# Recurrent layer, 2 slices of 1024 tokens on each of 8 cores: one half's norm beside the other half's products, two sums written out for quadrant 12, s and x fetched in fours, and TensorE on zeros at the start

## The reference

```python
x = L0_attn_x
xn = _layernorm(x, axis=-1)
s = _L0_attn_ref(xn, L0_attn_input_weights, L0_attn_xis, L0_attn_proj_matrix)
g = _silu(_L0_ffn_ref(xn, ...))
x = x + s * g

def _L0_attn_ref(x, input_weights, xis, proj_matrix):
    def _rfs(xw, ab, AB, gs):
        dot_products = jnp.einsum('...d,rd->...r', xw, ab[:, None] * gs)
        correction = (0.5 * jnp.sum(xw * xw, axis=-1))[..., None] * (ab * ab)
        return 1.0 / math.sqrt(NUM_RFS) * AB * jnp.exp(dot_products - correction)
    ab = xis
    AB = jnp.exp(xis)
    weights = _rfs(input_weights, ab, AB, proj_matrix)
    feats = _rfs(x, ab, AB, proj_matrix)
    return jnp.einsum('bsr,or->bso', feats, weights)

def _L0_ffn_ref(x, w1_w, w1_s, w2_w, w2_s, h1_w, h1_s, h2_w, h2_s, w3_w, w3_s):
    h = jax.nn.silu(_tlin(x, w1_w, w1_s)) * _tlin(x, w2_w, w2_s)
    h = jax.nn.gelu(_tlin(h, h1_w, h1_s), approximate=False)
    h = jax.nn.gelu(_tlin(h, h2_w, h2_s), approximate=False)
    return _tlin(h, w3_w, w3_s)
```

## Time and profile before

| | |
|---|---|
| median of 3 runs | 2441.12 us (2439.59 to 2442.6) |
| the profiled execution | 2439.11 us |
| its span on the slowest core, core 4 | 2438.0 us |
| spans of the eight cores | 2417.9 to 2438.0 us |
| busy: PE, DVE, ACT, POOL | 2358.3, 1118.9, 416.8, 220.8 us |

### The profile page before, as it was taken

The page is one execution under the profiler, slowest core; times in us unless marked ns, Lnnn a source line. Parts: engine busy times, 40 slices in busy tenths (PEclk is TensorE's granted clock), DMA queues, the critical chain, the costliest instruction groups (busy, mean ns, idle before and its releaser), DMA issues.

```text
span 2438.0 us, 29505 instructions; the slowest of 8 cores (2417.9 to 2438.0 us)
## 1 busy us (share of the span) xinstructions
PE 2358.3 (97%) x10832; PEld 1062.0 (44%) x10832; DVE 1118.9 (46%) x1269; ACT 416.8 (17%) x589; POOL 220.8 (9%) x390
## 2 busy tenths in 40 slices
PE   6999999999999999999799999999999999999968
PEld 2444444444444444444344444444444444444423
DVE  4433443444744444563640433444443744343556
ACT  2212111111111111112422222111111111111111
POOL 1000000000000001011030000000000000000000
PEclk8999999999999999999999999999999999999989
DMA  7543455555655555678411643465656564656675
GB/s 139 95 79 69 72 92 92 93 91 95 119 86 99 95 90 99 128 136 125 109 70 70 104 75 65 74 103 82 106 81 105 105 107 81 106 82 103 124 172 121
DMA packets 78717, 240.01 MB, mean 98 GB/s; under 512 B 8304, under 2 KB 20208, under 8 KB 77552
## 3 DMA queue, kind: packets, MB, share of 16 engines
q0 software_dynamic: 57120, 192.96, 49.4%
q1 hardware_dynamic: 21456, 45.17, 5.8%
HBM read 408.49 MB, written 22.54 MB: 177 GB/s over the span
## 4 chain that ended last, share of the span: by engine, by line
PE 89%; DVE 6%; DMA 3%; ACT 1%; issue 1%; SPq 0%; DVEq 0%; ACTq 0%; POOLq 0%
PE pb L157 86%; PE pb L316 2%; DMA blk<-s_hbm 2%; DVE tmp L605 1%; DMA wring<-w3p 1%; ACT blk L609 1%; DVE blk L259 1%; DVE blk L253 1%; DVE wring L352 1%; SPq L742 0%; DVE blk L481 0%; DVE blk L501 0%; DVE blk L475 0%; DMA blk<-xT 0%; DVE blk L628 0%
## 5 line engine op out<-in xcount | busy, mean ns | idle before, releaser
L157 PE MATMUL pb<-blk,wring 128*128 128x512 bf16 x9856 | 2133.3, 379 | 29.8 <-DVE wring L352 18.8
L157 PEld LDWEIGHTS pb<-blk,wring 128*128 128x128 bf16 x9856 | 964.4, 98 | 1198.4 <-issue 40.6
L352 DVE TENSOR_TENSOR wring<-wring 128x2048 bf16<-128x2048 bf16 x216 | 264.7, 1226 | 50.6 <-DVE tmp L411 16.5
L297 DVE SCALAR_TENSOR_TENSOR blk<-pb,cols,stg 128x512 bf16<-128x512 f32 x128 | 96.0, 750 | 291.7 <-PE pb L157 208.5
L359 DVE TENSOR_TENSOR wring<-wring 128x2048 bf16<-128x2048 bf16 x144 | 176.4, 1225 | 15.4 <-DVE blk L501 0.5
L452 ACT ACTIVATE blk<-pb,cols 128x512 bf16<-128x512 f32 x64 | 44.0, 687 | 680.2 <-DVE tmp L404 680.2
L157 PE MATMUL pb<-blk 128*128 128x512 bf16 x640 | 140.9, 383 | 17.1 <-ACT blk L609 17.1
L452 ACT ACTIVATE blk<-tmp,cols 128x512 bf16<-128x512 f32 x128 | 92.4, 722 | 350.1 <-DVE tmp L411 175.9
L292 ACT ACTIVATE stg<-pb,cols 128x512 bf16<-128x512 f32 x128 | 88.0, 688 | 337.2 <-PE pb L157 298.7
L183 POOL DMA_DIRECT2D wring<-h1p x128 | 67.9, 531 | 740.2 <-PE pb L157 740.2
L183 POOL DMA_DIRECT2D wring<-h2p x128 | 67.9, 531 | 710.2 <-PE pb L157 688.2
(11 more groups left out here) (67 smaller groups left out, 512.1 us busy)
## 6 DMA issues: line engine op xcount, KB each, us to landing
wring<-h1p POOLq DMA_DIRECT2D x128, 512.0 KB, 5.8
wring<-h2p POOLq DMA_DIRECT2D x128, 512.0 KB, 6.0
wring<-w12p POOLq DMA_DIRECT2D x64, 512.0 KB, 5.7
wring<-w3p POOLq DMA_DIRECT2D x32, 512.0 KB, 9.3
blk<-xT SPq DMA_DIRECT2D x32, 256.0 KB, 6.1
y<-blk SPq DMA_DIRECT2D x32, 256.0 KB, 2.5
blk<-xT POOLq DMA_DIRECT2D x16, 256.0 KB, 17.8
s_hbm<-blk SPq DMA_DIRECT2D x16, 256.0 KB, 2.1
```

The source lines that it names most:

```text
L157: ii = t.matmul(p[bk], lhs, rhs, start=(not onto and i == 0), stop=(i == n - 1), skip_group_check=onto)
L297: a = V(lambda: v.scalar_tensor_tensor(kt(h[q], row), p[b2], w2s_c[:, oc:oc + 1], stg[:, ts_, :], op0=ALU.mult, op1=ALU.mult), m2, a)
L352: tok = V(lambda: v.tensor_add(wring[:, so, :], wring[:, slots[ka][0], :], wring[:, slots[kb][0], :]), *toks, slots[ka][1], slots[kb][1])
```

## The change

- *Norm at the start.* The three steps of `ln_scale` become `ln_mean`, `ln_var` and `ln_rstd`, and squares and statistics are called pair by pair. A new function `head0`, given to `w12_stage` for the first slice, interleaves the norm of half 1 with the first products of half 0: three chunks in four passes, each on the two tiles of xn that are there, then chunks 3 to 6 of half 0, then chunks 0 to 6 of half 1. The second slice has no special pass: all chunks go one by one.
- *PE on zeros.* `eb` is set to 0, and 24 matmuls on it run before x has landed.
- *Norm between the slices.* Half 0's center and divide stand beside the 128 products for the input weights, one operation for every two of them; half 1's statistics follow those products, and its center and divide stand beside the y products, one for each tile. The center writes to `stg`. s of the second slice is made half by half.
- *Quadrant 12.* A tile in `stg` is combined on the spot with quadrants 22 and 11 into its tiles of M3 and M6 (`sums_out`), and both go to HBM; the last two row groups write them straight to their blocks (`sums_here`). In the last row group two DMAs of 14 tiles each bring M6 (after the first unit) and M3 (after the second) back.
- *s5* is formed after quadrant 22 of a row group, not before.
- *End.* x and s come in groups of four tiles each, in the order of use; tile 14 is finished at once.

```diff
-        def ln_scale(th, f0, f1, f2):
+        def ln_mean(th, f0, f1, f2):
 
             bm, bv = ln[th, "banks"]
-            a = S(lambda: sc.activation(f1, p[bm], AF.Square), ln[th, "q"])
-            c = V(lambda: v.tensor_sub(f1, p[bv], f1), a)
+            ln[th, "f"] = (f0, f1, f2)
+            a = V(lambda: v.tensor_copy(f0, p[bm]), ln[th, "q"])
+            free_bank(bm, a)
+            ln[th, "m2"] = S(lambda: sc.activation(f1, f0, AF.Square), a)
...
+            def head_chunks(n, jj, banks_):
+
+                need(t, ln[0, "xn", jj])
...
+                for i in range(n):
+                    need(t, slots[key(i)][1])
...
+            first = head(chunk, head_chunks, gate) if head else 0
+            for i in range(first):
+                ch = chunk(i, 1)
+                gate(*ch)
+                give_slot(key(i), ch[5])
...
@@ row_group
             free_bank(ba, emit("12", r, p[ba], v2))
-            if nxt:
-                weight_sums(*nxt, "s5")
...
             t_free[2 * par] = emit("22", r, ta, a)
             if nxt:
+                weight_sums(*nxt, "s5")
                 weight_sums(*nxt, "s1")
@@ hidden_stage
+            def sums_out(r):
+
+                i = 2 * (r % 2)
+                a = V(lambda: v.tensor_sub(stg[:, i + 1, :], stg[:, i, :], kt(o22, r)),
+                      o_tok["12", r], o_tok["22", r], now(d_stg[i + 1]))
+                need(sy, a)
+                d_stg[i + 1].inc(sy.dma_start(spill[s_, nm, "M3"][:, r, :], stg[:, i + 1, :]), 16)
+                a = V(lambda: v.tensor_add(stg[:, i, :], stg[:, i, :], kt(o11, r)), o_tok["11", r])
+                need(sy, a)
+                d_stg[i].inc(sy.dma_start(spill[s_, nm, "M6"][:, r, :], stg[:, i, :]), 16)
...
-            def sum_m3():
-                V(lambda: v.tensor_sub(most(nb["M3"]), most(nb["M6"]), most(o22)),
-                  end["u1"], end["r12"])
...
+            def fetch(op, m):
+                need(sy, m, *[now(d) for d in d_stg])
+                reload_tok[op] = d_rel[op].inc(sy.dma_start(blk[:, nb[op], 0:14 * N], spill[s_, nm, op]), 16)
@@ the start
+        for _ in range(24):
+            t.matmul(p[7], ones_d, eb[:, 0, :], start=True, stop=True)
...
+        def head0(chunk, head_chunks, gate):
+
+            bk = []
+            head_chunks(3, 0, bk)
+            ln_stats(1, b_x, b_q, 3)
+            head_chunks(3, 1, bk)
+            ln_mean(1, *lnf[3:6])
+            ln_center(0, b_x, ft[0], 2)
+            ln_divide(0, b_xn, ft[0], 2)
+            ln_var(1)
+            ln_rstd(1)
+            head_chunks(3, 2, bk)
...
+            ch = head_chunks(3, 3, bk)
...
+            for jj in range(3):
+                c = chunk(3 + jj, 0)
+                if jj < 2:
+                    ln_center(1, b_x, ft[1], 2 + jj)
+                ln_divide(1, b_xn, ft[1], 1 + jj)
+                gate(*c)
+            gate(*chunk(6, 0))
@@ beside the input weights' products
-                    ln_center(rc // 4, b_x, ftl, rc % 4)
-                    ln_divide(rc // 4, b_xn1, ftl, rc % 4)
+                    if rc % 2 == 0:
+                        ln_center(0, b_x, ftl, rc // 2)
+                    else:
+                        ln_divide(0, b_xn1, ftl, rc // 2)
@@ the end
-                for n_ in range(8):
-                    x_load(n_, end["u4"])
-                need(sy, end["u5"], end["u6"], now(d_s))
-                sr = [d_sr[i].inc(sy.dma_start(f32b(b), s_hbm[:, 8 * i:8 * i + 8, :]), 16)
-                      for i, b in enumerate((fr1, fr2))]
+                def load(n0, x_after, s_after):
+
+                    need(sy, *x_after)
+                    for n_ in range(n0, n0 + 4):
+                        rows, cs, oc, th = where(*order[n_])
+                        d_xf[n_ % 8].inc(sy.dma_start(xf[:, n_ % 8, :], xT[rows, cs]), 16)
+                    need(sy, *s_after)
+                    for n_ in range(n0, n0 + 4):
+                        rows, cs, oc, th = where(*order[n_])
+                        in_tok[n_] = d_xf[n_ % 8].inc(
+                            sy.dma_start(sv[n_], s_hbm[:, 2 * oc + th, :]), 16)
+
+                in_tok = {}
+                load(0, [end["u4"]], [end["u5"], now(d_s)])
```

More of the change, by code:

```diff
@@ L111, in build_nc @@
         d_s = Ctr(nc, stack, "d_s")
-        d_sr = [Ctr(nc, stack, f"d_sr{i}") for i in range(2)]
         waited = {}
@@ L219, in ln_squares @@
             cs = slice(th * N, (th + 1) * N)
-            for jj in range(4):
-                js = slice(2 * jj, 2 * jj + 2)
-                ln[th, "sq", jj] = S(lambda: sc.activation(xq[:, js, cs], xb[:, js, cs], AF.Square),
-                                     ln[th, "x", jj], *toks)
-        def ln_stats(th, b, bq):
-            xb, xq = wide(b), wide(bq)
-            cs = slice(th * N, (th + 1) * N)
-            need(t, ones_tok)
-            bm, bv = take_bank(), take_bank()
-            for j in range(8):
-                need(t, ln[th, "sq", j // 2])
+            if jj == 0:
+                need(t, ones_tok)
+                ln[th, "banks"] = (take_bank(), take_bank())
@@ L337, in w12_stage @@
+            first = head(chunk, head_chunks, gate) if head else 0
[3 more added lines that the diff above has]
+                give_slot(key(i), ch[5])
+                if i % 2 == 1:
+                    sums(i // 2)
+            for i in range(first, 32):
+                for th in range(2):
+                    ch = chunk(i, th)
+                    gate(*ch)
+                give_slot(key(i), ch[5])
                 if i % 2 == 1:
@@ L485, in edge_last @@
                 if u == 0:
-                    need(sy, m, *[now(d) for d in d_stg])
-                    end["r12"] = d_rel.inc(sy.dma_start(most(nb["M6"]), spill[s_, nm][:, 0:15, :]), 16)
+                    fetch("M6", m)
+                elif u == 1:
+                    fetch("M3", m)
                 elif u == 2:
@@ L647, in build_nc @@
                     x_load(n_, s_, f_last)
-                ln_stats(0, b_x, b_q)
-                ln_stats(1, b_x, b_q)
+                for jj in range(4):
+                    ln_stats(0, b_x, b_q, jj)
                 need(t, iw_sq)
```

297 lines of the change are left out of this document (168 added, 129 removed).

## The result

The changed kernel takes **2403.35 us**, the median of four executions (2401.37, 2401.82, 2404.88 and one of 2688.45), and in the same session the kernel before takes 2441.86 (2439.59 to 2445.34). The ratio is **0.9838, 95% interval 0.9819 to 0.9858**: 1.6% faster. The range of 2379 to 2407 holds it; the forecast was 2392.5.

What follows compares the result with a forecast made beforehand. TensorE bounds the kernel: busy 97%, 2336.5 us of matmuls as floor, 101.5 us of waits or slow clock. Gains 8.3 + 23.7 + 0 + 15.4 + 1.2 = 48.6 gave 2390.5 profiled, 2392.5 median, range 2379 to 2407.

Steps and rivals of the forecast that it cites:

- head: Start of the first slice: half 0's products begin with its first norm tile; gain 8.3 us, bounds 5 to 12.
- middle: Between the two token slices: half the centers and divides move beside the y products; gain 23.7 us, 0.5 left.
- last stage: Second slice's w3: the wait for s goes, 7.4 us left of 22.8; gain 15.4 us, bounds 5 and 22.8.
- rival 2: Changes of stage: second reload is dear, fourth weight 8 us or more late; 2407 us in all, chance 0.17.
- a break above 8 us at a change of stage: Sign in the profile after that would make the sum wrong: PE breaks above 8 us where one stage follows another.
- h1 to h2: Change of stage, both slices: 2 us lost to the fourth weight where 1.7 and 2.0 were; net 0, twice.
- h2 to w3: Change of stage: first slice net 0, PE stopped 4.88 before; second slice 4.0 us idle plus 2.4 slow restart.
- tail: After the last products: two of four DVE steps of 0.7 to 0.9 us go; gain 1.2 us.
- Changes of stage: Four places: two block sums go, a second reload delays the fourth weight 4 to 5 us; gain 0.
- Rival 1: Changes of stage and last stage: the second reload costs nothing; 2380 us in all, chance 0.13.
- The rule against the row: Skill's two-port DVE rule, set aside: it would blame block sums for late fourth weights and make the second reload free.
- Rivals 3 and 4: 3: middle stays shut, 2410 us, chance 0.08; 4: chip withholds 2.4 GHz, slower than before, 2463 at 0.97, chance 0.03.

Runs made afterwards that it cites:

- the deferral: Changed kernel with xn's block and projT fetched after the third unit of w3's second row group, not at the end of h2; 2393.09 us.
- the spread kernel: Changed kernel with M3's reload after the fifth unit, xn and projT fetched in w3's second row group, s5 before quadrant 22 in the last stage alone; 2385.06 us.

## Why the prediction was right, and which terms were off

The sign and the range held, and the gains came where the prediction put them, in the head, the middle and the last stage; the sum was 11.3 us too fast (2401.8 against 2390.5). The range holds the result because it was drawn to take in rival 2. Of the signs named ahead, one of those against the sum came: a break above 8 us at a change of stage (9.56). By its own terms, on core 5 of after:

| term | left or gained by the prediction | in the trace | too fast by |
|---|---|---|---|
| head | gain 8.3 | 5.1 | 3.2 |
| middle | gain 23.7 | 24.2 | -0.5 |
| h1 to h2, first slice | 2 left | 2.74 + 1.9 slow | 2.7 |
| h1 to h2, second slice | 2 left | 0 | -2.0 |
| h2 to w3, first slice | 4.9 + 2.6 left | 9.56 + 2.9 slow | 5.0 |
| h2 to w3, second slice | 4.0 + 2.4 left | 6.33 + 2.9 slow | 2.8 |
| row groups of w3 | 1 left | 0.69 + 0.79 + 0.69 | 1.2 |
| tail | gain 1.2 | 0.5 | 0.7 |

That makes 13.1 for the 11.3; the 1.8 over is not accounted for, and the rows of before are core 4's, those of after core 5's. "Slow" is what a run of matmuls behind a stop takes over 0.2157 each: 94 in 22.14 (20.3 due), 121 in 28.95 (26.1), 112 in 27.04 (24.2).

**Changes of stage: the step that failed.** The prediction took 4 to 5 us for the second reload, "as part of the traffic is through by then", and nothing in the first slice's change to w3. The price is 6.5 us on the slowest cores (24.7 against 18.2) and 5.0 to 8.1 by the medians at the four changes. The second slice agrees: issued at 2272.48, landed at 2294.05, 21.6 us, where before the same weight took 15.3. For what the prediction said was through by then the trace has no sign: the DMA share is 1.02 in the window from 1015 to 1047, with 253 GB/s. 1.66 MB more in 6.5 us are 3.9 us for each MB.

The sum had priced the reload, which moves bf16 as it is, like weights, whose MB it counted in f32. The page of after has the two apart (queue, packets, MB as they land, share of 16 engines' span); POOL's casting transfers are q0, SP's are q1:

```profile
q0 software_dynamic: 57120, 192.96, 47.7%
q1 hardware_dynamic: 31536, 58.81, 7.5%
```

That is 5.9 us of all 16 engines for each MB that lands by q0 and 3.1 by q1 (2400.8 x 0.477 / 192.96 and x 0.075 / 58.81). An estimate from it is 1.66 x 3.1 = 5.1 us, the low end of what was measured. The prediction's 3.2 us for an MB is near the 3.1 only because a weight's MB of f32 lands as half an MB.

And xn's and projT's places were taken as given, while the deferral shows that their 4 MB make 7.5 of the 9.56 us (6.9 of 8.3 in the mean over the cores). Rival 2 (8 us late, 2407) was closer than the forecast, 3.7 us off against 10.9; the measurement lies between them. Rival 1 (free, 2380) is excluded.

**Head.** The chunks end at 44.36 instead of 41.1. The third weight came at 31.07, not 28.8, and the matmuls of that pass and the four of statistics behind it, 0.43 us apart, ran at the 1.2 GHz level (granted clock 0.50 from 31.0 to 34.4): eight of them cost 3.4 us. The prediction had put them "between the levels" and counted 2.7; PE had waited 1.90 and 1.17 us just before. The 256th matmul, with 80 done at 44.36, comes at 44.36 + 176 x 0.2157 = 82.3, against 87.4: 5.1 gained. Even that is much for this change, since core 4, from which the prediction read its 66.7, was the last of its run; the median of the cores is 64.6, and 43.3 stands for the 44.36 in after, so that the 256th moves from 85.3 to 81.2 only, 4.0. In the kernel with the old head it is at 84.6, and undoing the head costs 3.3.

**Middle.** As worked out: no stop at all, and the 0.5 left was not needed.

**Last stage.** The break for s is gone, as forecast; undoing it costs 14.8 for a gain put at 15.4 and 1.2 in the tail. The three stops of 0.7 to 0.8 are not weights that land late but order. On DVE, quadrant 22's L443 and the finishing L852 and L854 stand ahead of s5 from 2319.23 on; s5 runs from 2321.89, and PE, already waiting for it, goes on at 2323.26. With s5 ahead of quadrant 22 the three stops are gone.

**Tail.** The chain that ended last, last pieces (start, us, what):

```profile
2394.40 0.70 DVE blk L854
...
2395.26 0.70 DVE tmp L443
...
2396.05 0.73 ACT stg L866
...
2396.94 0.70 DVE blk L852
...
2397.74 0.69 DVE blk L854
```

PE ends at 2373.41 + 20.88 = 2394.29, but L443 waits until 2395.26 for tile 14's L852 and L854 ahead of it on DVE. From the end of PE to that of L854 it is 4.1 us (2398.4 - 2394.3), before 4.6 (2435.7 - 2431.1): 0.5 gained, not 1.2.

**The rule against the row.** The late weights follow the reloads and not DVE: with both reloads late the same weight landed in 5.8 us beside a block sum of 4.16. That DVE had been idle for 10.73 us before the L367 of 1044.83 would not show it alone, since two block sums (L519 and L522) ran in the 10 us behind the issue. The prediction was right to side with its row, but it took the rule further than the page does. The Trainium skill (SBUF — State Buffer, "SBUF: two separate sides") gives the rule for DVE operations in a two-port mode, and says in the same section that `tensor_tensor`, which the block sums are, has no such mode; the trace agrees. By that page they do not make the weight late, and the second reload is not free by it. What another page says agrees as well: by the Trainium skill (DMA: Bandwidth & Descriptors, "Issuing engines are not separate DMA queues") DMAs of SP and GpSimd run on the same 16 engines and interleave, and here 1.66 MB more on SP's queue made GpSimd's weight 6.5 us later (18.2 to 24.7).

**Rivals 3 and 4** did not come. The mean granted clock was 0.992 to 0.996 over the cores of the profiled execution, with all of them dense. That the cores would draw together came only in part: their spans lie 16.2 us apart, 20.1 before.

## What to carry to other kernels

Before adding a transfer, list what else is issued in the same 20 us and what the first consumer waits for: the bytes are cheap on average (a DMA share of 0.5) and dear where weights for a new stage, a reload and a prefetch meet. When an idea that removes stalls makes others, move its transfers and those of its neighbours before dropping it; two sums lost 6 us beside a 4 MB prefetch and an early second reload, and won 8.6 with both moved. Put a restart beside every stop of some microseconds, as a range: on core 5 of the changed kernel 1.9 to 2.9 us went to slow matmuls behind stops of 2.7 to 9.6, but none on cores 3 and 6 behind stops of 2.9.

## What the runs showed of the hardware that was not expected

- *A prefetch of 4 MB that nobody waits for* set the longest stop: 6.7 to 9.9 us by core with it, 0 to 2.9 with it deferred, and in the kernel with both reloads late 8.4 to 11.4 and none.
- *The cores fall in pairs.* In the profiled execution of the changed kernel cores 0 to 7 have spans of 2386.6, 2399.1, 2400.6, 2387.9, 2384.6, 2400.8, 2386.4 and 2398.2 us: in each pair (0 and 1, 2 and 3, ...) one is 12 to 16 us behind the other, and in other executions it is the other one (2403.2 and 2394.8 for cores 0 and 1). Now and then a pair stays together (2393.2 us for both cores 0 and 1 of the kernel with the deferral alone). Before, the pairs were 7 to 20 us apart; in the spread kernel they are 8 to 11. Most of the difference is in the stops for weights: core 0 stopped 2.30 us at the second slice's change to w3 where core 1 stopped 6.44, and 11.3 against 19.7 us at all four changes. No core waits for another in the program. By the Trainium skill (HBM Reference, "Specifications (TRN2)") the two cores of a pair share the bandwidth of their HBM, which would fit; no run here used one core of a pair alone, so it stays open.
- *Zeros ahead of the data.* With them the first sixteen statistics matmuls run 0.22 us apart, without them twelve at 0.43. But on core 5, 3.22 us of idle later, the next ones are 0.43 apart again, and the whole was worth nothing behind a weight that is awaited anyway.
